# One ring of single-head score banks in an attention phase

## The reference, cut to what matters

```python
sq = (x @ wq_s).reshape(b, n, S, DH).transpose(0, 2, 1, 3) * scale      # S = 8, DH = 16
sk = (x @ wk_s).reshape(b, n, S, DH).transpose(0, 2, 1, 3)
rv = (x @ wv_r).reshape(b, n, R, DH).transpose(0, 2, 1, 3)              # R = 2
search_attn = jax.nn.softmax(jnp.einsum('bsid,bsjd->bsij', sq, sk), axis=-1)
retrieved = jnp.einsum('bsij,brjd->bsird', search_attn, rv)
rk = retrieved @ wk_ret
retrieval_attn = jax.nn.softmax(jnp.einsum('bsid,bsird->bsir', rq, rk), axis=-1)
out = jnp.einsum('bsir,bsird->bsid', retrieval_attn, retrieved)
```

## Time and profile before

| | us |
|---|---|
| median of 3 runs | 5405.85 (5404.78 to 5411.82) |
| the profiled execution | 5417.14 |
| its span | 5415.5 |
| attention phase, from its first score to its last output, about | 1541 to 3652 of the span |
| PE busy, whole span | 4417.4 (82%) |
| DVE / ACT / POOL busy | 3040.9 (56%) / 2084.2 (38%) / 1818.9 (34%) |
| sum of `P` pairs on POOL (L1410) | x256, mean 4.523 |
| exponential of 512 (L1675) / of 1024 (L1670) | x1024, mean 0.596 / x512, mean 1.024 |

### The profile page before, as it was taken

The page is one execution under the profiler, slowest core; times in us unless marked ns, Lnnn a source line. Parts: engine busy times, 40 slices in busy tenths (PEclk is TensorE's granted clock), DMA queues, the critical chain, the costliest instruction groups (busy, mean ns, idle before and its releaser), DMA issues. The chain is left out here.

```text
span 5415.5 us, 71207 instructions
## 1 busy us (share of the span) xinstructions
PE 4417.4 (82%) x21775; PEld 1741.5 (32%) x21775; DVE 3040.9 (56%) x5454; ACT 2084.2 (38%) x3333; POOL 1818.9 (34%) x1328
## 2 busy tenths in 40 slices
PE   4499999984799888989898989975999999665423
PEld 2133333323322222222222222223444444343212
DVE  4777777765677676767666767716000000467663
ACT  3311111115435555555555555554444433413100
POOL 1000000004537776767666767773000000302101
PEclk9799999997879999999999999987999999856655
DMA  1343434425802222222222222102000000202304
GB/s 67 80 91 88 106 89 101 92 52 206 225 11 32 36 32 30 30 30 30 30 30 30 30 30 29 18 8 77 0 0 0 0 0 0 97 39 103 99 0 136
DMA packets 208208, 295.43 MB, mean 55 GB/s; under 512 B 43943, under 2 KB 136109, under 8 KB 206525
## 3 DMA queue, kind: packets, MB, share of 16 engines
q1 hardware_dynamic: 179768, 256.87, 21.6%
q10 hardware_dynamic: 23808, 25.17, 1.3%
q0 software_dynamic: 4368, 10.07, 0.6%
HBM read 94.49 MB, written 69.73 MB: 30 GB/s over the span
## 5 line engine op out<-in xcount | busy, mean ns | idle before, releaser
L1599 DVE TENSOR_REDUCE at_mx<-at_side 128x1 f32<-128x512 f32 x2048 | 1284.1, 684 | 390.8 <-PE at_side L1480 374.3
L1410 POOL TENSOR_TENSOR at_pairs<-at_P 128x2048 f32<-128x2048 f32 x256 | 1157.9, 4523 | 713.6 <-PE at_den L1546 605.6
L1675 ACT ACTIVATE at_P<-at_Sone 128x512 f32<-128x512 f32 x1024 | 610.6, 596 | 555.0 <-PE at_Sone L1508 553.6
L1480 PE MATMUL at_side<-at_ko,at_qo 96*128 96x512 bf16 x2048 | 724.2, 401 | 61.7 <-DMA at_ko<-qk 23.5
L1670 ACT ACTIVATE at_P<-at_Spair 128x1024 f32<-128x1024 f32 x512 | 524.3, 1024 | 274.9 <-PE at_Spair L1508 176.8
L1535 PE MATMUL at_num<-at_P,at_rvt 128*32 128x512 f32 x4096 | 562.5, 622 | 0.0
L1508 PE MATMUL at_Sone<-at_qo,at_ko 99*128 99x512 bf16 x1024 | 402.8, 393 | 193.1 <-ACT at_P L1675 163.3
L1952 ACT ACTIVATE ff_hs<-ff_ph,ff_b 128x512 f32<-128x512 f32 x512 | 351.6, 687 | 524.1 <-PE ff_ph L1922 524.1
L1922 PE MATMUL ff_ph<-ffn_Y,ff_w 128*128 (+1 forms) x1024 | 524.4, 594 | 8.6 <-DMA ff_b<-in_b_dram 8.6
L1936 PE MATMUL ff_po<-ff_hs,ff_w2s 128*128 128x512 f32 x1024 | 522.5, 592 | 0.0
L616 PE MATMUL la_acc<-la_rep,la_wagg 128*32 128x512 f32 x4096 | 511.2, 606 | 1.2 <-DMA la_rep<-la_pad 1.1
(11 more groups left out here) (412 smaller groups left out, 4937.4 us busy)
## 6 DMA issues: line engine op xcount, KB each, us to landing
la_rep<-la_pad SPq DMA_DIRECT2D x512, 162.2 KB, 3.6
qk<-ap_part SPq DMA_DIRECT2D x32, 768.0 KB, 3.7
at_qo<-qk SPq DMA_DIRECT2D x192, 128.0 KB, 4.7
at_ko<-qk SPq DMA_DIRECT2D x192, 128.0 KB, 7.6
n_ln_xs<-X SPq DMA_DIRECT2D x96, 256.0 KB, 2.3
u<-ap_us SPq DMA_DIRECT2D x32, 320.0 KB, 4.0
X<-in_x_dram SPq DMA_DIRECT2D x4, 2048.0 KB, 21.2
proj<-la_y POOLq DMA_DIRECT2D x32, 256.0 KB, 2.3
```

The source lines that it names most:

```text
L1410: g.tensor_tensor(pairs[:, :, :], P[a][:, :, :], P[a + 1][:, :, :], ALU.add).then_inc(pair_done, 1)
L1480: return pe.matmul(side[bank][:, :], qo[1 - u][0:KQ, s, i * C:(i + 1) * C], ko[1 - u][0:KQ, s, h * CH:(h + 1) * CH], start=True, stop=True)
L1599: v.reduce_max(mx[:, n // 2, n % 2:n % 2 + 1], side[bank][:, :], AX.X).then_inc(side_saved, 1)
L1675: a.activation(P[k % SLOTS][:, 2 + i, :], Sone[:, :], ACT.Exp).then_inc(p_ready, 1)
```

## The change

The names `Spair` and `Sone` go. Three single banks `S0` to `S2` form a ring: head n = 4k + i of a slot goes to bank n mod 3, and each score raises `s_ready` by itself (128 a slot in place of 96). Each exponential has 512 columns, four a step, and raises `p_ready`. PE issues all four heads of step k+2 in step k, each followed by a quarter of the side work; none of step k+1 is left for step k. The save moves behind the second exponential of its step. The thresholds on SP and POOL are the old points in the new counts, except SP's later load, which waits for 96 of 128 heads as it waited for 72 of 96. `values`, `totals`, `pair`, `retrieve` and `drain` are otherwise as before.

```diff
-        Spair = m.ps("Spair", [C, 2, CH])
-        Sone = m.ps("Sone", [C, CH])
+        S = [m.ps(f"S{u}", [C, CH]) for u in range(RING)]
...
-                    g.wait_ge(p_ready, 96 * b + 6 * i + 6)
+                    g.wait_ge(p_ready, HEADS * b + 8 * i + 8)
...
-                def scores01(b, u, k):
-                    wait_if(pe, p_ready, 96 * b + 3 * k - 2)
...
-                def scores3(b, u, k):
-                    pe.wait_ge(p_ready, 96 * b + 3 * k + 2)
-                    score(b, u, k, 3, Sone[:, :]).then_inc(s_ready, 1)
+                    h, n = QUAD * quad + i, 4 * k + i
+                    wait_if(pe, p_ready, HEADS * b + (n - 2 if n >= RING else n - 1 if n < 2 else -2))
+                    pe.matmul(S[n % RING][:, :], ko[u][:, h, j * C:(j + 1) * C], qo[u][:, h, half * CH:(half + 1) * CH],
+                              start=True, stop=True).then_inc(s_ready, 1)
...
-                        if k + 1 < STEPS:
-                            scores3(b, u, k + 1)
...
-                        for part in range(3):
-                            for w in work[cuts[part]:cuts[part + 1]]:
+                        for i in range(QUAD):
+                            if ahead_of:
+                                score(*ahead_of, i)
+                            for w in work[(i * len(work) + 2) // 4:((i + 1) * len(work) + 2) // 4]:
                                 fill(w, b, u, side_free(b, at), at % SIDES).then_inc(side_ready, 1)
                                 at += 1
-                            if part == 0 and ahead_of:
-                                scores01(*ahead_of)
-                            if part == 1 and ahead_of:
-                                scores2(*ahead_of)
                         values(b, u, k)
...
-                    a.wait_ge(s_ready, 96 * b + 3 * k + 1)
-                    a.activation(P[k % SLOTS][:, 0:2, :], Spair[:, :, :], ACT.Exp).then_inc(p_ready, 1)
-                    if saved:
-                        save(*saved)
-                    for i in range(2):
-                        a.wait_ge(s_ready, 96 * b + 3 * k + 2 + i)
-                        a.activation(P[k % SLOTS][:, 2 + i, :], Sone[:, :], ACT.Exp).then_inc(p_ready, 1)
+                    for i in range(QUAD):
+                        if saved and i == 2:
+                            save(*saved)
+                        a.wait_ge(s_ready, HEADS * b + 4 * k + i + 1)
+                        a.activation(P[k % SLOTS][:, i, :], S[(4 * k + i) % RING][:, :], ACT.Exp).then_inc(p_ready, 1)
```

More of the change, by code:

```diff
@@ L1205, in _ @@
                 mids(NCH - 1, R - 1)
-STEPS = 32
 MAX_UNITS = 128
@@ L1211 @@
 SLOTS = 4
+STEPS = 32
 SIDES = 3
+RING = 3
+HEADS = STEPS * 4
 TOKENS_AT = (2, 18)
@@ L1374, in slot @@
                     if not last and not is_first(b):
-                        sp.wait_ge(s_ready, 96 * b)
+                        sp.wait_ge(s_ready, HEADS * b)
                         load(b + 1, 1 - u, 1)
@@ L1391, in slot @@
                     if not isinstance(b, int) or b < B - 2:
-                        sp.wait_ge(s_ready, 96 * b + 72)
+                        sp.wait_ge(s_ready, HEADS * b + 96)
                         load(b + 2, u, 0)
@@ L1502, in fill, with score @@
                     return pe.matmul(side[bank][:, :], wout[:, :], oc[:, :], start=True, stop=True)
-                def score(b, u, k, i, out):
+                def score(b, u, k, i):
                     g, j = divmod(k, 8)
                     half, quad = divmod(g, 2)
-                    h = QUAD * quad + i
-                    return pe.matmul(out, ko[u][:, h, j * C:(j + 1) * C], qo[u][:, h, half * CH:(half + 1) * CH],
-                                     start=True, stop=True)
-                def scores01(b, u, k):
-                    wait_if(pe, p_ready, 96 * b + 3 * k - 2)
[L1514 to L1521, removed]
-                def scores3(b, u, k):
-                    pe.wait_ge(p_ready, 96 * b + 3 * k + 2)
-                    score(b, u, k, 3, Sone[:, :]).then_inc(s_ready, 1)
+                    h, n = QUAD * quad + i, 4 * k + i
+                    wait_if(pe, p_ready, HEADS * b + (n - 2 if n >= RING else n - 1 if n < 2 else -2))
+                    if k in (0, 8) and i == 0:
+                        pe.wait_ge(row_in[u][quad], rows_count(b, u))
+                    pe.matmul(S[n % RING][:, :], ko[u][:, h, j * C:(j + 1) * C], qo[u][:, h, half * CH:(half + 1) * CH],
+                              start=True, stop=True).then_inc(s_ready, 1)
                 def values(b, u, k):
@@ L1532, in values @@
                         wait_if(pe, num_saved, 4 * b + g)
-                    pe.wait_ge(p_ready, 96 * b + 3 * k + 3)
+                    pe.wait_ge(p_ready, HEADS * b + 4 * k + 4)
                     for i in range(QUAD):
@@ L1559, in slot @@
                     if first:
[L1560 to L1564, removed]
+                        for n in range(8):
+                            score(b, u, n // 4, n % 4)
                     for k in range(STEPS):
@@ L1568, in slot @@
                         work = side_work(k, first, last)
-                        cuts = [0, (len(work) + 1) // 4, (3 * len(work) + 1) // 4, len(work)]
-                        if k + 1 < STEPS:
-                            scores3(b, u, k + 1)
-                        elif not last:
-                            scores3(b + 1, 1 - u, 0)
                         ahead_of = (b, u, k + 2) if k + 2 < STEPS else None if last else (b + 1, 1 - u, k + 2 - STEPS)
-                        for part in range(3):
-                            for w in work[cuts[part]:cuts[part + 1]]:
+                        for i in range(QUAD):
+                            if ahead_of:
+                                score(*ahead_of, i)
+                            for w in work[(i * len(work) + 2) // 4:((i + 1) * len(work) + 2) // 4]:
                                 fill(w, b, u, side_free(b, at), at % SIDES).then_inc(side_ready, 1)
                                 at += 1
-                            if part == 0 and ahead_of:
-                                scores01(*ahead_of)
-                            if part == 1 and ahead_of:
-                                scores2(*ahead_of)
                         values(b, u, k)
```

## The result

The changed kernel takes 5452.65 us (median of 4 runs, 5451.36 to 5453.94) against 5408.84 for the kernel before on the same chip. The ratio is 1.0081, with a 95% interval from 1.0064 to 1.0099: it is slower by 43.8 us. 44 were forecast, and 5450.

A forecast was written before the change was run, and what follows sets the result against it. PE bound the attention phase; the new order closes a ring through POOL and ACT. Loop 33.6, slots 1 and 14 5.6, slot 0 7.4, slot 15 15.9, clock -18.5: +44, 5450 us; range 5404 to 5500.

The forecast's parts named there:

- The order on PE: Head 3 of step k+2 now goes before step k's values and totals; a quiet pair of steps pays 1.40 us.
- the ring: Totals, POOL's sum, ACT's exponential, PE's fourth score, next totals: at least 7.94 us from totals to totals (T to T).
- The pairs one by one: Half slot by pairs: save +0.13 each, quiet +1.40 each, tokens unchanged, wout -0.35, rows -1.5 us; a slot +2.8.
- rival 1: Side banks stop limiting too: rows, token, back and wout pairs fall towards 7.94 us; 5414 us, chance 0.12.
- Rival 3: POOL's ring doesn't bind; saves, rows pairs and clock gain: -89 us, 5317 us, chance 0.08.
- slots 1 to 14, clock included: Loop 33.6 us, slots 1 and 14 5.6, less 18.5 for the half clock: +20.7 us.
- slot 0: No work behind it: six quiet pairs, four saves of other pairs and one rows pair, +7.4 us.
- slot 15: No maximum tiles: its 14 pairs go from 6.59 to 7.72 us each, +15.9 us.
- start of the phase, tail: Time before the first totals and behind the last ones: forecast 0.
- the second rival: PE's clock falls to half in the ring's wait, in every fourth of some 220 pairs: 5546 us, chance 0.12.
- The loop's turn: PE's idle 8.34 us at the loop's turn: unchanged, within 1 us a turn.
- The clock behind `rows`: The 13 half-clock windows of 3.4 us behind the rows fill go with the last of its waits: -18.5 us.

The follow-up runs named there:

- two_sums: The changed kernel with two buffers for the sum of pairs (back tile and wout moved to make room): 5302.14 us, 0.9799 of before.
- late_fourth: The changed kernel with the fourth head of step k+1 issued in step k again, as before the change: 5343.57 us, 0.9878 of before.
- save_end: The changed kernel with the save behind the fourth exponential of its step, not the second: 5448.61 us, 1.0074 of before.
- two_sums_before: The control: the kernel before with two buffers for the sum of pairs and the same room made: 5406.43 us, 0.9997 of before.
- before_rows19: The kernel before with the first of its two rows jobs moved from step 17 to step 19: 5410.39 us, 0.9998 of before.

## Why the prediction was right, point by point

**The order on PE and the ring, T to T 7.94: right, to 0.01.** T + 1.24, T + 5.87, T + 6.53 and T + 7.95 were measured for 1.24, 5.87, 6.53 and 7.94. Two cuts at different places, two_sums and late_fourth, each open it; the control shows that the buffer by itself is worth nothing.

**The pairs one by one.** Save pairs 7.94 (7.94 forecast; 8.00 from step 30 to the next 0), quiet 7.93 to 7.95 (7.94), wout pair 8.79 (8.77), `rows` pairs 8.57 to 8.77 (8.4). Too low by 0.2 there: I had the save in it and DVE's queue a little short, and save_end shows that DVE alone sets it. Pairs with tokens were forecast unchanged at 8.03 and came down to the ring's 7.94, the longest from 9.33 to 8.90: a small part of rival 1, from where the tiles now stand. Rival 3, that the ring doesn't bind, is excluded by the measured quiet pairs; its price of -89 was near what two_sums then gave, -108.

**The sum, by its terms**, profiled execution against profiled execution, from totals to totals:

| | forecast | measured |
|---|---|---|
| slots 1 to 14, clock included | +20.7 | +9.0 |
| slot 0 | +7.4 | +7.0 |
| slot 15 | +15.9 | +23.5 |
| start of the phase, tail | 0 | -4.6, +1.8 |
| sum, span | +44 | +36.7 |
| medians of the runs | +44 | +43.8 |

The sum was met more closely than its parts, and that is luck: the first four rows were off by -12, 0, +8 and -3, which leaves the span 7 us under the forecast, and the medians then moved 7 us more than the profiled executions. In slots 1 to 14 the token pairs gave back 10.3 us where I had nothing; quiet pairs cost 77.6 for 78.4, and the `rows` pairs with their clock gave 61.9 for 60.5. In slot 15 I had the ring right (7.62 where the clock was full, 7.72 forecast) and the clock wrong. There PE has no tiles, idles more of each pair, and half clock comes in four windows between 3551 and 3599 (the first is shown) and again at 3626 and 3650, in a slot that had none before its end; pairs that a window touches take 8.1 to 8.6. That is the second rival, at the one place where PE has least to do, and worth some 8 us. The stretch that I took for its absence, rows 7's last line, ends at 2402.50, where half clock begins (2402.50 to 2405.90): it was weak evidence. Nor are such windows proof of the ring's wait, as two_sums_before has some in slot 15 without it. The loop's turn was left at nothing, and the pairs across it are 16.7 to 17.1 where they were 16.1 to 17.5.

**The clock behind `rows`.** The 13 windows are gone, as forecast, but the cause that I gave, two saves and then the wait for the bank, is not shown: before_rows19 keeps all three at step 1 and has one window there in place of six. The price of 18.5 was read from one execution, and two_sums_before suggests that it varies. What removes them stays open. In the runs here, the three kernels that have such windows in the loop are those whose `rows` pair takes 10.0 at full clock; where it takes 8.6 to 9.7 there is none. That goes together and is not shown to be the cause. Of the exponentials I said that four of 512 cost nothing; two_sums, which keeps them, has quiet pairs of 6.55 for 6.54.

The rule of the Trainium skill that I weighed ("TensorE: Matmul & The Clock Gate", "A second HAM failure mode: psum-queue depth-cycling") fits slot 15 alone: waits for exponentials of 25.1 us in 14 pairs, and a clock that falls and rises. In the loop's slots the same three banks are cycled with a wait of 1.23 us in the quiet pair shown, and no such window comes.

Rivals 1 and 3 count 27 `rows` pairs; slots 0 to 14 have 29, which moves their prices by 1 to 3 us.

## What to carry to other kernels

Working further ahead on one engine can close a ring through the others: before issuing a piece earlier, follow its wait back to where it comes round to this engine's own later work, and add up the durations. A stall's price is what it is worth after the next bound: the same move of the save gave 4 us with the ring closed, 88 with it open, and 152 in the kernel before (half-clock windows that went with it included). Put work that waits for the engine being fed (a copy out of its last result) behind everything that this engine needs next.

## What the runs showed that I had not expected

The granted clock's short falls are not tied to one wait. Kernels whose medians agree within 0.1% had 13, 9 and 1 windows of 3.4 us in the loop's slots, partly at different places, though PE's order was the same or one job had moved by two steps. So the clock's share of a time is a range and not a number that one execution gives: the kernel before was profiled at 5417.14, and its runs in all groups go from 5400.85 to 5424.14. In slot 15 the changed kernel had six such windows and save_end five, where the kernels with the ring cut had none before the slot's end; that two_sums_before had some too leaves it open what brings them.
